# Row maxima of the attention layer started inside the hyperbolic pass, with masks in eight places of their own and the targets sent in two halves

## The reference, cut to what matters

```python
support_t = adj @ x_tangent                       # hyperbolic layer
h = proj(expmap0(support_t, C_IN), C_IN)
xt = jax.nn.relu(logmap0(h, C_IN))
...
h = x @ W.T                                       # attention layer
a_src = (h * attn_src).sum(axis=-1)
a_dst = (h * attn_dst).sum(axis=-1)
scores = a_src[None, :] + a_dst[:, None]
mask = (adj > 0).astype(h.dtype)
s = jnp.where(scores > 0, scores, ALPHA * scores) * mask
s = s - jnp.max(s, axis=1, keepdims=True)
e = jnp.exp(s) * mask
w = e / (jnp.sum(e, axis=1, keepdims=True) + 1e-08)
out = w @ h
```

## Time and profile before

| | |
|---|---|
| median of 3 runs | 2944.71 us |
| lowest, highest | 2942.32, 2945.97 us |
| the profiled execution | 2943.5 us |
| its span | 2941.7 us |
| PE, DVE, ACT, POOL busy | 75%, 69%, 51%, 3% of the span |

### The profile page before, as it was taken

How to read it: one execution, slowest core, us unless ns; L and a number is a source line. 1 busy time by engine, 2 the same in 40 slices (tenths; PEclk the granted TensorE clock), 3 DMA queues, 4 the chain that set the end, 5 groups by cost and what they waited for, 6 DMA issues and landing times.

```text
span 2941.7 us, 20195 instructions
## 1 busy us (share of the span) xinstructions
PE 2200.8 (75%) x5939; PEld 952.6 (32%) x5939; DVE 2026.0 (69%) x2428; ACT 1501.7 (51%) x1447; POOL 99.4 (3%) x152
## 2 busy tenths in 40 slices
PE   4665444444789999999988399920089995999998
PEld 3222111111334444444433244410033332444443
DVE  7986899888679888889956644569799995000000
ACT  1005888888767777777736523310088883100000
POOL 1001100100100000000000000000000000000000
PEclk9757777776899999999998699965599997999999
DMA  7999888887633223233130088737766662989895
GB/s 259 387 389 336 302 319 328 322 312 289 251 127 101 100 100 129 100 104 109 60 143 0 1 287 278 256 119 226 273 217 229 214 228 98 304 299 305 299 312 168
DMA packets 176772, 638.37 MB, mean 217 GB/s; under 512 B 11776, under 2 KB 16176, under 8 KB 133296
## 3 DMA queue, kind: packets, MB, share of 16 engines
q1 hardware_dynamic: 161408, 572.86, 56.5%
q0 software_dynamic: 15280, 64.47, 5.5%
HBM read 597.24 MB, written 40.04 MB: 217 GB/s over the span
## 4 chain that ended last, share of the span: by engine, by line
PE 60%; DVE 16%; issue 14%; ACT 4%; SPq 3%; DMA 3%; DVEq 1%; POOL 0%; ACTq 0%; POOLq 0%
PE bank L584 22%; PE bank L749 15%; PE bank L709 8%; DVE arena L1342 8%; PE bank L657 8%; SPq L264 2%; PE bank L714 2%; DVE arena L1321 1%; DVE arena L1205 1%; PE bank L572 1%; DMA arena<-in_adj 1%; PE bank L604 1%; DVE arena L1130 1%; PE bank L549 1%; PE bank L605 1%
## 5 line engine op out<-in xcount | busy, mean ns | idle before, releaser
L584 PE MATMUL bank<-arena 128*128 128x512 f32 x1536 | 661.6, 594 | 13.3 <-DVE arena L1427 13.3
L549 PE MATMUL bank<-arena 128*128 128x512 f32 x512 | 258.7, 668 | 294.2 <-ACT arena L851 233.7
L749 PE MATMUL bank<-arena 128*128 128x512 f32 x1024 | 443.4, 594 | 29.6 <-ACT arena L1082 29.6
L1342 DVE CUSTOM_DVE_ANT_0 arena<-arena 128x2048 f32<-128x2048 bf16 x192 | 435.5, 2317 | 28.0 <-ACT arena L844 17.2
L1427 DVE TENSOR_TENSOR arena<-arena 128x2048 f32<-128x2048 f32 x192 | 433.2, 2282 | 4.0 <-ACT arena L888 2.1
L844 ACT ACTIVATE arena<-arena,nmx 128x2048 f32<-128x2048 f32 x192 | 384.5, 2002 | 72.8 <-DVE nmx L1342 58.6
L584 PEld LDWEIGHTS bank<-arena 128*128 128x128 f32 x1536 | 292.6, 191 | 382.1 <-issue 381.9
L888 ACT ACTIVATE arena<-arena 128x2048 f32<-128x2048 f32 x128 | 244.5, 1911 | 142.7 <-DVE arena L1416 142.7
L1659 DVE TENSOR_TENSOR arena<-arena,bank 128x512 f32<-128x512 f32 x8 | 5.3, 686 | 416.3 <-PE bank L731 416.3
L749 PEld LDWEIGHTS bank<-arena 128*128 128x128 f32 x1024 | 194.2, 191 | 269.6 <-issue 239.7
L709 PE MATMUL bank<-arena 128*128 128x512 f32 x512 | 238.9, 610 | 24.8 <-DVE arena L1627 24.8
(11 more groups left out here) (232 smaller groups left out, 2093.2 us busy)
## 6 DMA issues: line engine op xcount, KB each, us to landing
arena<-in_adjT SPq DMA_DIRECT2D x384, 1024.0 KB, 5.2
arena<-in_adj SPq DMA_DIRECT2D x128, 1024.0 KB, 5.1
mask_d<-arena POOLq DMA_DIRECT2D x64, 512.0 KB, 7.0
arena<-mask_d SPq DMA_DIRECT2D x64, 512.0 KB, 3.7
arena<-e_d POOLq DMA_DIRECT2D x6, 1024.0 KB, 11.7
arena<-nm_d POOLq DMA_DIRECT2D x6, 1024.0 KB, 7.0
arena<-gat_d POOLq DMA_DIRECT2D x6, 1024.0 KB, 6.7
arena<-in_x SPq DMA_DIRECT2D x4, 512.0 KB, 6.8
```

The source lines that it names most:

```text
L549: last = pe.matmul(banks[2][:], H[:, t, :], groups[4 + g % 4][:, b, :], start=(t == 0), stop=(t == T - 1))
L584: last = pe.matmul(banks[B * half + b][:], hW[:, t, h * C:(h + 1) * C], probs[k % 4][:, b * CH:(b + 1) * CH], start=(t == 0 and h == 0), s ...
L749: last = pe.matmul(banks[B * half + b][:], stationary[:, t, :], ring[slot][:, b * CH:(b + 1) * CH], start=(t == 0), stop=(t == T - 1))
L1342: v.tensor_tensor_reduce(logits[k % 3], mask, e_row, FAR_UNIT, FAR, ALU.add, ALU.min, nmx[:, k:k + 1]).then_inc(S["logits_ready"], 1)
```

## The change

- The masks get eight places of 4 KB per partition of their own, at R + 56 and on, that the hyperbolic pass doesn't use. POOL loads them, in five batches between its other work; SP's queue has only the adjT tiles left.
- After chunk 3 DVE makes the source column of the first 16 tiles, PE turns it in chunk 5 after group 0, ACT copies it in chunk 4's work, POOL stores and broadcasts it. The second half follows after chunk 7.
- DVE makes four maxima after normalising chunk 5, four after chunk 6, five after chunk 7, before it takes up the logit columns of that chunk. The other 51 follow after the pass.
- After maximum 47 the targets of the first 16 tiles are complete: their columns are made, turned, copied, stored (two DMAs), and broadcast, while DVE makes the last 16 maxima. The second half follows those, and ACT copies its rows between the first and the second slopes.
- The loops of the pass are written out on PE, ACT and DVE.

The diff, cut to its core:

```diff
-    used = [8 * p + 8 * (p > PASS_MAX) for p in range(6)]
+    used = [8 * p + 8 * (p > PASS_MAX) - 8 * (p > PASS_GATMAX) for p in range(6)]
...
-        not_positive = [at(8 * slot, HALF, dt=BF16) for slot in range(G)]
+        not_positive = [at(R + o, HALF, dt=BF16) for o in (56, 60, 64, 68, 72, 76, 98, 102)]
+        src_rows, dst_rows = at(R + 106, P)[0:T // 2, :], [at(R + 80 + 0.5 * i, P)[0:T, :] for i in range(2)]
...
+        dst_cols = [sb(f"dst_cols{i}", [P, 2, T // 2]) for i in range(2)]
...
+        EARLY = 10
...
-                    sp.wait_ge(S["even_mask_stored"], 16 * (STEPS // 2))
-                    sp.wait_ge(S["odd_mask_stored"], 16 * (STEPS // 2))
-                    for n in range(STEPS):
-                        sp.wait_ge(freed[n % G], n // G + used[p] + 1)
-                        sp.dma_start(not_positive[n % G], mask_d[n]).then_inc(loaded[n % G], 16)
...
-            pool.wait_ge(S["gat_rows_ready"], 1)
-            pool.dma_start(gat_d[0:T, :], rows[0:T, :]).then_inc(S["gat_rows_stored"], 16)
-            pool.wait_ge(S["gat_rows_stored"], 16)
-            for half, signal in enumerate(("src_broadcast", "src_second_broadcast")):
+            def load_masks(first, end):
+                for n in range(first, end):
+                    if n >= G:
+                        pool.wait_ge(S["mask_used"], n - G + 1)
+                    pool.dma_start(not_positive[n % G], mask_d[n]).then_inc(mask_loaded[n % G], 16)
+
...
+                rows_of = slice(half * (T // 2), (half + 1) * (T // 2))
+                pool.wait_ge(S["gat_rows_ready"], half + 1)
+                pool.dma_start(gat_d[rows_of, :], src_rows).then_inc(S["gat_rows_stored"], 16)
+                pool.wait_ge(S["gat_rows_stored"], 16 * (half + 1))
                 pool.dma_start(src_bc[:, half * HALF:(half + 1) * HALF],
-                               gat_d[half * (T // 2):(half + 1) * (T // 2), :].rearrange("t p -> (t p)").partition_broadcast(P))\
-                    .then_inc(S[signal], 16)
-            pool.wait_ge(S["gat_rows_ready"], 2)
-            pool.dma_start(gat_d[T:3 * T, :], rows[0:2 * T, :]).then_inc(S["gat_rows_stored"], 16)
-            pool.wait_ge(S["gat_rows_stored"], 32)
-            dst_v = gat_d[T:3 * T, :].rearrange("(h t) p -> h (t p)", h=2)
-            for piece, signal in ((slice(0, HALF), "first_dst_loaded"), (slice(HALF, N), "dst_loaded")):
+                               gat_d[rows_of, :].rearrange("t p -> (t p)").partition_broadcast(P)).then_inc(S[signal], 16)
...
+                pool.wait_ge(S["gat_rows_ready"], half + 3)
+                for h in range(2):
+                    first = T * (1 + h) + half * (T // 2)
+                    pool.dma_start(gat_d[first:first + T // 2, :], dst_rows[half][h * (T // 2):(h + 1) * (T // 2), :])\
+                        .then_inc(S["gat_rows_stored"], 16)
+                pool.wait_ge(S["gat_rows_stored"], 64 + 32 * half)
+                dst_v = gat_d[T:3 * T, :].rearrange("(h t) p -> h (t p)", h=2)
+                piece = slice(half * HALF, (half + 1) * HALF)
                 for h in range(2):
                     pool.dma_start(dst_all[h][:, piece], dst_v[h, piece].partition_broadcast(P)).then_inc(S[signal], 16)
...
+            pool.wait_ge(S["even_mask_stored"], 16 * (STEPS // 2))
+            pool.wait_ge(S["odd_mask_stored"], 16 * (STEPS // 2))
+            pool.wait_ge(S["tangent_ready"], G)
+            load_masks(0, G)
+            spread_sources(0, "src_broadcast")
+            load_masks(G, G + EARLY)
+            spread_sources(1, "src_second_broadcast")
+            load_masks(G + EARLY, T + T // 2 + G)
+            spread_targets(0, "first_dst_loaded")
+            load_masks(T + T // 2 + G, STEPS)
+            spread_targets(1, "dst_loaded")
...
+            def turn_sources(half):
+                pe.wait_ge(S["src_cols_ready"], half + 1)
+                pe.transpose(banks[2][0:T // 2, 0:P], s[:, 9, half * (T // 2):(half + 1) * (T // 2)], ident[:])\
+                    .then_inc(S["src_cols_turned"], 1)
+
+            def turn_targets(half):
+                pe.wait_ge(S["gat_max_done"], half + 1)
+                pe.transpose(banks[2][0:T, 0:P], dst_cols[half].rearrange("p a t -> p (a t)"), ident[:])\
+                    .then_inc(S["dst_cols_turned"], 1)
...
                 for g in range(G):
+                    if q == B + 1 and g == 1:
+                        turn_sources(0)
...
-            with pe.Fori(1, Q) as q:
+            for q in range(1, Q):
                 hyperbolic(q, False)
...
-            pe.wait_ge(S["gat_cols_turned"], 1)
-            pe.transpose(banks[2][0:T, 0:P], s[:, 9, :], ident[:]).then_inc(S["gat_cols_turned"], 1)
-            pe.wait_ge(S["gat_max_done"], 1)
-            pe.transpose(banks[2][0:2 * T, 0:P], s[:, 4:6, :].rearrange("p a t -> p (a t)"), ident[:])\
-                .then_inc(S["gat_cols_turned"], 1)
+            turn_sources(1)
+            turn_targets(0)
+            turn_targets(1)
...
-            with act.Fori(0, Q) as q:
-                for c, per in ((roots, 2), (tanhs, 2), (logs, 1)):
-                    c.enter(q, per)
+            def source_rows(half):
+                act.wait_ge(S["src_cols_turned"], half + 1)
+                if half:
+                    act.wait_ge(S["gat_rows_stored"], 16)
+                act.activation(src_rows, banks[2][0:T // 2, 0:P], ACT.Copy).then_inc(S["gat_rows_ready"], 1)
...
+            def target_rows(half):
+                act.wait_ge(S["dst_cols_turned"], half + 1)
+                act.activation(dst_rows[half], banks[2][0:T, 0:P], ACT.Copy).then_inc(S["gat_rows_ready"], 1)
+
+            for q in range(Q):
                 evacuate(q, PASS_HYP, 0)
...
+                if q == B:
+                    source_rows(0)
...
-            for c in (roots, tanhs, logs):
...
-            act.wait_ge(S["gat_cols_turned"], 2)
-            act.activation(rows[0:T, :], banks[2][0:T, 0:P], ACT.Copy).then_inc(S["gat_rows_ready"], 1)
-
-            act.wait_ge(S["gat_cols_turned"], 3)
-
-            act.wait_ge(S["gat_rows_stored"], 16)
-            act.activation(rows[0:2 * T, :], banks[2][0:2 * T, 0:P], ACT.Copy).then_inc(S["gat_rows_ready"], 1)
+
+            source_rows(1)
+            target_rows(0)
             act.wait_ge(S["first_dst_loaded"], 32)
...
             slopes(0)
+            target_rows(1)
             slopes(1)
...
-            with dve.Fori(0, Q) as q:
...
+            ts(sc(3), dg[:], 0.0, -1.0, ALU.is_gt, ALU.mult)
...
+            def row_maxima(count):
...
+                for _ in range(count):
+                    n = maxima_made[0]
+                    half, t, g = n // T, n % T, n % G
+                    if n == 0:
+                        dve.wait_ge(S["src_broadcast"], 16)
+                    if n == T:
+                        dve.wait_ge(S["src_second_broadcast"], 16)
+                    dve.wait_ge(mask_loaded[g], 16 * (n // G + 1))
+                    if t // (T // 2) == half:
+
+                        d = not_positive[g][:, t % (T // 2) * P:(t % (T // 2) + 1) * P]
+                        ch(v.scalar_tensor_tensor(d, ident[:], sc(3)[:, t:t + 1], d, ALU.mult, ALU.add))
+                    if n >= 2:
+                        dve.wait_ge(S["mask_used"], n - 1)
+                    v.tensor_tensor_reduce(masked_src[n % 2], not_positive[g], src_bc[:, half * HALF:(half + 1) * HALF],
+                                           FAR_UNIT, FAR, ALU.add, ALU.min, sc(4 + half)[:, t:t + 1]).then_inc(S["mask_used"], 1)
+                    maxima_made[0] += 1
+
+            def source_columns(half):
+                tiles = slice(half * (T // 2), (half + 1) * (T // 2))
+                ch(v.tensor_scalar(sc(8)[:, tiles], sc(0)[:, tiles], SLOPE, None, ALU.mult))
+                v.tensor_scalar(sc(9)[:, tiles], sc(0)[:, tiles], -NEAR_UNIT, None, ALU.mult).then_inc(S["src_cols_ready"], 1)
+
+            for q in range(Q):
                 dve.wait_ge(S["chunk_stored"], q + 1)
...
                 normalise(2, q, h4)
+                if q > B:
+                    row_maxima((EARLY - 1) // 2 + (1 if q == Q - 1 else 0))
                 dve.wait_ge(S["mx_copied"], q + (G + 1))
...
-            ts(sc(9), sc(0), -NEAR_UNIT, None, ALU.mult)
-            v.tensor_scalar(sc(8), sc(0), SLOPE, None, ALU.mult).then_inc(S["gat_cols_turned"], 1)
-            ts(sc(3), dg[:], 0.0, -1.0, ALU.is_gt, ALU.mult)
-            dve.wait_ge(S["src_broadcast"], 16)
-
-            for half in range(2):
-                if half:
-                    dve.wait_ge(S["src_second_broadcast"], 16)
-                for t in range(T):
-                    g = t % G
-                    dve.wait_ge(loaded[g], 16 * (used[PASS_GATMAX] + B * half + t // G + 1))
-                    if t // (T // 2) == half:
...
-                    n = T * half + t
-                    if n >= 2:
-                        dve.wait_ge(freed[(n - 2) % G], used[PASS_GATMAX] + (n - 2) // G + 2)
```

(23 more changed lines are left out.)

33 lines of the change are left out of this document (13 added, 20 removed).

## The result

| | before | after |
|---|---|---|
| median of the runs | 2943.52 us (4 runs) | 2895.86 us (4 runs) |
| lowest, highest | 2938.29, 2945.97 | 2894.29, 2903.62 |
| the profiled execution | 2943.5 | 2897.1 |
| its span | 2941.7 | 2894.5 |

The ratio is 0.9845, with an interval of 0.9831 to 0.9859: 45.6 us faster by the ratio, 47.7 by the medians. The forecast was 2901 from 2944.7, 43.4 less, with a range of 2894 to 2915. It was right.

The account below looks back on a forecast made before the run. TensorE bounds the hyperbolic pass, DVE alone the row maxima after it, then the target chain. Terms 1.5 + 13.0 + 3.7 + 120.3 + 5.1 + 8.5 = 152.1 us replace 195.5, 43.4 less: 2901 us, range 2894 to 2915.

Parts of the forecast that it names:

- overrun: In the pass, four maxima overfill DVE's holes, so the next chunk starts 0.75 us late, twice: 1.5 us, bounds 1.2 and 3.
- five maxima: After the last normalised chunk DVE takes five maxima, 13.0 us, covering the hole of 4.82 us before the columns.
- columns: Logit columns and source columns on DVE at the end of the pass: 3.7 us.
- 51 maxima and target columns twice: After the pass: remaining maxima 120.3 us; two sets of target columns 5.1 us, 2.55 of them new.
- start of the attention: From the last target columns to the first attention matmul: ACT's row copy 0.9 plus 7.6, together 8.5 us.
- the 8.23: DVE's hole before the first maximum, 8.23 us, closed because the first half of the sources is sent during the pass.
- Mask 18: Queued on POOL behind the second source row and broadcast; taken as hidden, 0 us of wait, range 0 to 1.1.
- The port: Rival: POOL's load issues stop DVE, up to 0.53 us a mask, 29 us back, 2930 us; chance 0.04.
- The starved pass: Rival: mixed DMA queues are less efficient and TensorE waits up to 13 us in the pass, 2905 to 2914; chance 0.10.
- The mask stream: Rival: POOL's queue brings a mask only every 3.5 us from mask 18 on, +53 us, 2954; chance 0.03.
- It doesn't do what it says: Rival: late source row holds the pass, or other mishaps eat the moved maxima's 21 us; 2922 us; chance 0.05.
- Before the first and after the second I expect the same course.: Outside the stretch from last normalised chunk to first attention matmul, 195.5 us before the change, nothing was expected to change.

Follow-up runs that it names:

- before_unrolled: The kernel before with the loops of PE, ACT and DVE over the pass's chunks written out, nothing else; 2936.79 us, ratio 0.9987.
- none_in_pass: The kernel after with no maxima before the logit columns of any chunk, all 64 taken after the pass; 2924.54 us, ratio 0.9942.
- targets_late: The kernel after with the first half's target columns made after all 64 maxima and sent after all masks; 2909.31 us, ratio 0.9893.
- after_again: The kernel after, run again unchanged; 2902.32 us, ratio 0.9868.
- from_chunk_four: The kernel after with the first source row sent earlier and four maxima after chunk 4 too, 17 before the last logit columns; 2891.36 us, ratio 0.9828.
- before_masks_from_pool: The kernel before with its 64 mask loads issued by POOL instead of SP, into the same places; 2945.47 us, ratio 1.0015.
- tail_five_only: The kernel after with only the five maxima after chunk 7, none after chunks 5 and 6; 2922.3 us, ratio 0.9937.
- before_more_semaphores: The kernel before with eleven unused semaphores more; 2939.17 us, ratio 0.9998.
- chunk_four_split: from_chunk_four with masks 23 to 63 loaded by SP after its first eight attention tiles; 2888.22 us, ratio 0.982.
- after_padded: The kernel after with 128 idle semaphore increments at the head of PE's program; 2919.54 us, ratio 0.9926.

## Why the prediction was right

**The sum.** From the last normalised chunk to the first matmul of the attention it had 195.5 - 43.4 = 152.1 us with the overrun of 1.5, so 150.6 from the chunk itself. Measured: 1940.76 to 2090.18, 149.4, and 45.4 us less on D. Term by term, in us:

| step | forecast | measured, from |
|---|---|---|
| overrun of chunks 5 and 6 | 1.5 | 0.9 (30.61 + 30.60 - 2 x 30.15) |
| five maxima | 13.0 | 13.0 (1940.79 to 1953.79) |
| columns | 3.7 | 3.2 (1953.79 to 1956.97) |
| 51 maxima and target columns twice | 120.3 + 5.1 | 124.7 (1956.97 to 2081.69) |
| start of the attention | 8.5 | 8.5 (2081.69 to 2090.18) |

The parts of the chain have the size that was forecast. D is 2.0 us shorter than forecast: 0.6 on the overrun, 0.5 on the columns, 0.7 on the target columns, and 0.2 because DVE's way from the last matmul to the last normalised chunk is shorter (20.15 us before, 19.98 in before_unrolled).

**The overrun** is a term that was mis-sized, by 0.6. The bounds of 1.2 to 3 didn't hold it. The forecast set 10.4 us of maxima against 8.27 + 1.48 of idle time in the old trace, and added 0.1 for waits, of which there were none. With the loops written out the two holes are 8.08 + 1.92 = 10.00 (before_unrolled) and 9.99 (chunk 5 of none_in_pass), a quarter of a microsecond more: DVE's way through a chunk became 0.44 shorter, PE's period 0.15 to 0.2. The forecast had set the written-out loops at nothing, 1 either way, since the trace shows no pause at a loop's turn; they gave 1.1 us in the pass and shortened DVE's own steps in D by some 0.5. (D as a whole is 215.6 in before_unrolled, for its source and its target broadcasts landed later, by 0.4 us each.) That four maxima fill the holes, that three leave time lying and that a fifth gains nothing, is what the other two sizes showed. DVE's delay reached PE in no chunk, as argued: up to its last matmul the pass of after has no wait of PE for the normalised chunk.

**The maxima inside the pass** are worth 19.9 us with what they cost (forecast 20.8 - 1.5 = 19.3), those after chunk 7 are worth 4.7 (4.82). **The first half's sources** sent early remove the 8.23. **The first half's targets** are worth 9.8 against targets_late; against the kernel before the chain is 24.7 - 10.7 - 2.2 = 11.8 shorter (forecast 13.6 - 2.55 = 11.1), since in targets_late the store had landed 1.8 sooner than there. So 19.9 + 4.7 + 8.2 + 11.8 = 44.6 of the 45.4 are named. Most of the rest lies ahead of the first maximum: none_in_pass has 8.30 from the start of the layer norm's last step to it (1940.84 to 1949.14), before had 17.24, which is 8.94 less with a hole of 8.23; the source and logit columns took 3.2 us where they had taken 3.7. A set of target columns, half as wide, took 2.2 us (2079.47 to 2081.69) where the forecast charged 2.55.

**Waits that were set at nothing.** Mask 18 was there: no idle time stands before any maximum. One reading was off: the first source row took 5.0 us from its store to its broadcast (1839.21 to 1844.21; 4.7 in after_again), not 2.5, in a pass at a DMA share of 0.90. It had a whole chunk, and in from_chunk_four, where it was sent 5.2 us earlier in its chunk (2.1 us after the squares instead of 7.3), it took 2.0. The second took 1.9 (1958.23 to 1960.12), and so mask 18 was issued at 1960.76, 3.8 us after maximum 13 began. For the DMA engines the forecast counted 31 us of extra work in the pass, 6 more than was free. The share over 1700 to 1925 went from 0.83 to 0.92 (after_again), some 20 us, so the pass had room.

**The rivals.** *The port* (2930) counted 55 masks loaded from the last chunk on; they are 48, since 16 of the 64 are issued before its maxima, so its price was 25 us and not 29. It fell: the source view of the minima (shortest, median, longest ns) has in the kernel after

```profile
L1593 DVE CUSTOM_DVE_ANT_0 arena<-arena x64: 2283/2288/2293, 1880.0 to 2077.3; 128x2048 f32<-128x2048 bf16 x64
```

a spread of 10 ns over 64 minima, most with an issue of POOL beside them, and before_masks_from_pool has the same mean. The Trainium skill (SBUF — State Buffer, "Who interferes with whom") ties the starving of GpSimd's DMAs to two-port modes of DVE. No starving was seen here, with 0.53 us an issue, and whether this minimum is such a mode no run shows. *The starved pass* (2905 to 2914) fell twice: a share of 0.93 and 0.97 in after, 0.94 throughout in from_chunk_four, PE busy 29.6 of 30.3. A mask took 4.7 us to land in the median where 7 had been feared, and the lead of over 20 us carried the rest. *The mask stream* (2954) fell by the same row: 4.7 us with up to eight under way is far from 3.3 a mask. *It doesn't do what it says* (2922) is what tail_five_only and none_in_pass look like, 2922.3 and 2924.5, and the kernel run beside them (2902.3) is 20 us from both.

**What failed.** "Before the first and after the second I expect the same course." Three things moved outside. The pass is 0.9 us shorter (241.9 and 241.0): 1.1 by the loops, less 0.2 for PE's extra transpose. The clock in the GRU stage gave the first profiled execution 3.8 us before the pass began (first matmul at 1679.7 against 1683.5); that comes and goes between runs of one kernel and is not the change. And the end of the program grew by 3.4 us in every run of the kernel after, which the forecast, in moving 64 loads from SP to POOL and adding four DMAs of its own, had costed only by what waits behind them. In the execution with the same clock state, after_again, the account closes: ahead of the pass -0.4 (1683.5 to 1683.1), the pass -0.9, D -45.4, from the attention's first matmul to the last addition +0.7 (789.9 to 790.6), the end +3.5, together the -42.5 between the spans. That the forecast's 43.4 came out so near is partly luck: its own part was 2 us too small, the pass gave 0.9 that it had not, and the end, which it left out, took 3.5 back.

## What to carry to other kernels

Fill a hole with as much moved work as it holds, and read its size in a run of the new kernel that leaves it empty, and the period there too: here the holes are 9.99 us and four maxima 10.4, three left time lying and a fifth was worth nothing. A neighbouring chunk can mislead: chunk 4 has holes of 10.20 us, for the change put a transpose of PE's into it. A chain of small transfers (columns, transpose, store, broadcast) can be hidden by splitting its input in two and sending the first half while the bounding engine works on the second. Compare stages between fixed events and not whole times, for a clock granted elsewhere in the program can move the whole by more than a small effect: 4 us here, where a fourth maximum is worth 2.

## What was not expected of the hardware

**More DMAs on POOL's queue lengthen the end of the program.** From POOL's last issue to the end of the span (timelines of before and of after_again, the last issue of each, with the spans of 2941.7 and 2899.2):

```profile
2935.74 0.75 POOL L452 DMA_DIRECT2D out_x<-arena  x1 [0.36 <-issue]
```
```profile
2888.21 0.75 POOL L476 DMA_DIRECT2D out_x<-arena  x1 [0.64 <-issue]
```

| run | DMAs of POOL beyond before | last issue to the end of the span, us |
|---|---|---|
| before | 0 | 2935.74 to 2941.7: 6.0 |
| before_more_semaphores | 0 | 2930.72 to 2936.7: 6.0 |
| chunk_four_split | 27 | 2877.12 to 2885.4: 8.3 |
| before_masks_from_pool | 64 | 2930.39 to 2941.0: 10.6 |
| after_again | 68 | 2888.21 to 2899.2: 11.0 |
| after_padded | 68 | 2903.11 to 2914.1: 11.0 |

That is 0.07 to 0.09 us for each DMA more. Some 1.5 us comes back just ahead of it: from the last addition to the last issue it takes 4.7 us before (2931.0 to 2935.74), 3.2 in after_again (2885.0 to 2888.21) and 2.8 in chunk_four_split. That moving loads to POOL's queue does it is shown by before_masks_from_pool, where only the queue changed. Nearly all the DMAs moved are of one size, 512 KB, so their number and their bytes or packets grow together, and which of these counts no run here tells. By what means, and why the stores of the output issue more quickly, stays open too.

**The clock granted in a half-idle stage differs from run to run**: 0.60, 0.66 or 0.72 in the window 1620 to 1650 of the GRU, whose instructions the change doesn't touch. The whole stage, from its first matmul to the first of the hyperbolic pass, took 178.1 us (after, 0.72), 181.4 (tail_five_only, 0.66) or 183.1 (after_again, 0.60). One window doesn't tell it all: before_masks_from_pool had 0.60 there and took 179.7.
